# Two gated scan-and-experts layers: residual sums and normalisation statistics of the first five stages, VectorE's part given to TensorE and ScalarE

## What is computed

```python
x = x + tanh(g_xattn[0]) * scan0(ctx, layernorm(x))       # z gate = silu(layernorm(x))
x = x + tanh(g_ffn[0])   * experts(layernorm(x))          # 16 experts, 4 per row, and a shared one
x = x + tanh(g_xattn[1]) * scan1(ctx, layernorm(x))
x = x + tanh(g_ffn[1])   * lora(layernorm(x))

def layernorm(x, eps=1e-5):
    m, v = mean(x, -1), var(x, -1)
    return (x - m) / sqrt(v + eps)

# scan, for each of 512 channels and 16 states, along the 512 rows:
state = state * exp(d_t * A) + (d_t * u_t) * B_t;  y_t = sum_n state * C_t
y = (y + D * u) * silu(z)
# shared expert: silu(x @ gate.T) * (x @ up.T) @ down.T
```

## Time and profile before

| | |
|---|---|
| median of three runs | 1532.84 us |
| the profiled execution | 1534.31 us, its span 1532.5 us |
| VectorE busy | 1408.3 us, 92% |
| TensorE busy | 1270.7 us, 83% |
| ScalarE busy | 837.6 us, 55% |
| GpSimd busy | 786.1 us, 51% |
| TensorE's mean granted clock | 0.949 of full speed |

### The profile page before, as it was taken

How to read it: one execution, slowest core, us unless ns; L and a number is a source line. 1 busy time by engine, 2 the same in 40 slices (tenths; PEclk the granted TensorE clock), 3 DMA queues, 4 the chain that set the end, 5 groups by cost and what they waited for, 6 DMA issues and landing times.

```text
span 1532.5 us, 14502 instructions
## 1 busy us (share of the span) xinstructions
PE 1270.7 (83%) x4518; PEld 723.1 (47%) x4518; DVE 1408.3 (92%) x1468; ACT 837.6 (55%) x1344; POOL 786.1 (51%) x411
## 2 busy tenths in 40 slices
PE   6786787799689867986889999889988888836998
PEld 3321232343244324442456666566665666625555
DVE  5899999999999999998899999999899999987894
ACT  5755657464766455634865655647556444424442
POOL 0465456545544553450464555654556656555642
PEclk9898899999989998998999999999999999967999
DMA  7354445445543543451256768676786768754531
GB/s 251 103 135 128 111 130 143 130 120 143 139 139 92 145 130 107 96 165 29 83 177 239 236 239 273 231 273 236 248 258 231 280 268 280 247 191 141 169 106 56
DMA packets 99836, 264.30 MB, mean 172 GB/s; under 512 B 10832, under 2 KB 11344, under 8 KB 93616
## 3 DMA queue, kind: packets, MB, share of 16 engines
q1 hardware_dynamic: 87936, 225.36, 47.9%
q0 software_dynamic: 11440, 37.50, 7.3%
q10 hardware_dynamic: 384, 0.52, 0.1%
HBM read 233.73 MB, written 29.62 MB: 172 GB/s over the span
## 4 chain that ended last, share of the span: by engine, by line
DVE 41%; PE 24%; issue 8%; DMA 7%; POOL 5%; ACT 2%; DVEq 0%; SPq 0%; another core or an unknown queue 0%; ACTq 0%; POOLq 0%
DVE state L1663 18%; DVE banks L1655 11%; PE banks L1137 7%; DMA expert_w<-in_moe_w 3%; PE banks L1148 3%; PE banks L1047 3%; PE banks L1096 2%; DVE y_scan L1674 2%; DMA ys_d<-expert_out 2%; POOL state L451 2%; PE banks L1301 2%; PE banks L1104 1%; DVE hidden L1681 1%; DVE du L1375 1%; DVE small L1429 1%
## 5 line engine op out<-in xcount | busy, mean ns | idle before, releaser
L451 POOL TENSOR_TENSOR state<-state,bc_rows 128x1024 f32<-128x1024 f32 x254 | 599.0, 2359 | 641.9 <-DVE banks L1655 641.7
L1047 PE MATMUL banks<-state,ident 128*128 128x512 f32 x640 | 329.4, 645 | 115.5 <-POOL state L451 115.3
L1663 DVE TENSOR_TENSOR_SCAN state<-decay,banks 128x1024 f32<-128x1024 f32 x176 | 402.1, 2285 | 6.3 <-ACT decay L681 1.7
L1655 DVE TENSOR_TENSOR banks<-du,bc_rows 128x1024 f32<-128x1024 f32 x256 | 314.7, 1229 | 12.8 <-issue 0.5
L1137 PE MATMUL banks<-z_gate,expert_w 128*128 128x256 f32 (+1 forms) x1504 | 285.3, 348 | 7.6 <-DMA expert_w<-in_moe_w 7.3
L1137 PEld LDWEIGHTS banks<-z_gate,expert_w 128*128 128x128 f32 x1504 | 250.0, 191 | 60.8 <-issue 20.8
L681 ACT ACTIVATE decay<-delta,neg_a 128x511 f32<-128x511 f32 x352 | 230.8, 713 | 53.1 <-DVE state L1663 47.9
L1047 PEld LDWEIGHTS banks<-state,ident 128*128 128x128 f32 x640 | 118.3, 198 | 295.1 <-POOL state L451 184.3
L1663 DVE TENSOR_TENSOR_SCAN state<-expert_w,banks 128x1024 f32<-128x1024 f32 x80 | 182.9, 2286 | 8.5 <-ACT expert_w L681 5.9
L1148 PE MATMUL banks<-expert_w,hidden 128*128 128x512 f32 x316 | 155.2, 606 | 2.9 <-DVE hidden L1684 2.9
L1674 DVE TENSOR_TENSOR y_scan<-y_scan,state 128x1024 f32<-128x1024 f32 x94 | 113.9, 1212 | 3.1 <-POOL state L451 3.1
(11 more groups left out here) (313 smaller groups left out, 1622.8 us busy)
## 6 DMA issues: line engine op xcount, KB each, us to landing
bc_rows<-bc_d SPq DMA_DIRECT2D x208, 512.0 KB
expert_w<-in_moe_w SPq DMA_DIRECT2D x48, 1536.0 KB, 9.2
ys_d<-expert_out SPq DMA_DIRECT2D x32, 512.0 KB, 10.5
ctx_t<-in_ctxT SPq DMA_DIRECT2D x8, 512.0 KB, 6.8
x_res<-in_x SPq DMA_DIRECT2D x4, 1024.0 KB, 10.8
xn_d<-y_scan SPq DMA_DIRECT2D x4, 1024.0 KB, 7.5
ys_d<-expert_out SPq DMA_DIRECT2D x15, 256.0 KB, 9.3
out_x<-x_res SPq DMA_DIRECT2D x3, 1024.0 KB, 6.0
```

The source lines that it names most:

```text
L451: nc.gpsimd.tensor_tensor(W[:, c % 4], W[:, c % 4], bcast2(BC[:, u, 1, :]), ALU.mult).then_inc(mulc_done, 1)
L1047: mm = nc.tensor.matmul(PS[:, m], ID[:, :], W[:, c % 4, m, :], start=False, stop=True, skip_group_check=True)
L1655: nc.vector.tensor_tensor(drive(s), DU[:, s % 2, 2 * h:2 * h + 2, :], bcast2(BC[:, u, 0, :]), ALU.mult).then_inc(mulb_done, 1)
L1663: nc.vector.tensor_tensor_scan(flat(W[:, c % 4]), flat(DAS[c % da_slots(s, i)]), flat(drive(s)), 0.0, ALU.mult, ALU.add).then_inc(scan_don ...
```

## The change

- **TensorE adds the residual.** `y_transposes` becomes `scan_transposes` in stages 1 to 4: for each row tile an identity matmul puts the row tile of `x` into the bank, and four matmuls with the scan output as weights and `GID` (the identity times tanh of the gate) add the gated, transposed scan on top. `shared_out` likewise begins with an identity matmul of `x`; the shared expert's last weights are scaled by half the gate once, in place (`shw_ready`).
- **ScalarE copies out.** `scan_rows` copies each bank to `x` with a row sum as second output, scales the sums to negative means, and squares `x - mean` with a row sum of squares: the variance. It stands after c=5 and c=7 of the first quarter, ahead of `conv_tap(p, 1)` at c=5. `shared_rows` copies the shared banks to `x`, after c=0 and c=3 of the second quarter (stages 2, 3); in stage 4 after c=0 and c=2 of the second, and c=0 and c=2 of the third.
- **Input statistics.** `input_sums` (third quarter, c=0 and c=2), `mean` and `squares` (c=5, c=6) make those of the new batch.
- **VectorE** loses `scan_add`, `stats` and `shared_add` in these stages. `norm_bias` becomes a product for them, and EPS and 1/D go into `rstd_log` as bias and scale.

```diff
             def rstd_log(v):
                 act.wait_ge(var_ready, v + 1)
-                nc.scalar.activation(RS[:, :], RS[:, :], ACT.Ln).then_inc(std_step, 1)
+                nc.scalar.activation(RS[:, :], SQ[:, v % 2, :], ACT.Ln, scale=1.0 / D, bias=EPSC[:, :]).then_inc(std_step, 1)
+            def mean(v, lo, hi):
+                means[0] += 1
+                act.wait_ge(summed, means[0])
+                m = NMEAN[:, v % 2, lo:hi]
+                nc.scalar.activation(m, m, ACT.Copy, scale=-1.0 / D).then_inc(mean_ready, 1)
+            def squares(v, b, qs):
+                act.wait_ge(mean_ready, means[0])
+                for q in qs:
+                    ins = nc.scalar.activation(ZS[:, q, :], X[:, b * QT + q, :], ACT.Square, bias=NMEAN[:, v % 2, q:q + 1],
+                                               accum_out=SQ[:, v % 2, q:q + 1])
+                if q == QT - 1:
+                    ins.then_inc(var_ready, 1)
+            def input_sums(s, qs):
...
+                for q in qs:
+                    ins = nc.scalar.activation(ZS[:, q, :], X[:, s * QT + q, :], ACT.Copy, accum_out=NMEAN[:, 0, q:q + 1])
...
+            def scan_rows(f, lts):
+                for lt in lts:
+                    act.wait_ge(yt_done, QT * f + lt + 1)
+                    nc.scalar.activation(X[:, f * QT + lt, :], AUX[lt % 2], ACT.Copy,
+                                         accum_out=NMEAN[:, 1, lt:lt + 1]).then_inc(xacc, 1)
+                act.wait_ge(xacc, QT * f + lt + 1)
+                m = NMEAN[:, 1, lts[0]:lts[-1] + 1]
+                nc.scalar.activation(m, m, ACT.Copy, scale=-1.0 / D).then_inc(rows_mean, 1)
+                act.wait_ge(rows_mean, 2 * f + lts[-1] // 2 + 1)
+                for lt in lts:
+                    ins = nc.scalar.activation(ZS[:, lt, :], X[:, f * QT + lt, :], ACT.Square, bias=NMEAN[:, 1, lt:lt + 1],
+                                               accum_out=SQ[:, 1, lt:lt + 1])
...
+            def shared_rows(b, qs):
+                for q in qs:
+                    act.wait_ge(shdown_done, QT * b + q + 1)
+                    nc.scalar.activation(X[:, b * QT + q, :], AUX[q % 2], ACT.Copy).then_inc(shacc, 1)
...
+                    if c == 5 and f >= 0:
+                        scan_rows(f, (0, 1))
                     if c == (5 if f >= 0 else 6):
                         conv_tap(p, 1)
+                    if c == 7 and f >= 0:
+                        scan_rows(f, (2, 3))
...
                         decay(s, i, c)
+                        if i == 1 and c == 0 and g >= 0:
+                            shared_rows(g, (0, 1))
                         if i == 1 and c == 1:
                             silu_pair(p, 1)
+                        if i == 1 and c == 3 and g >= 0:
+                            shared_rows(g, (2, 3))
...
+                        if i == 2 and c in (0, 2):
+                            input_sums(s, (c, c + 1))
+                        if i == 2 and c == 5:
+                            mean(2 * s, 0, QT)
+                            squares(2 * s, s, (0, 1))
+                        if i == 2 and c == 6:
+                            squares(2 * s, s, (2, 3))
...
                 decay(s, 1, c)
+                if c == 0:
+                    shared_rows(f - 1, (0, 1))
                 if c == 1:
                     norm(f, XN)
+                if c == 2:
+                    shared_rows(f - 1, (2, 3))
...
+            def scan_transposes(f, y, lts):
+                pe.wait_ge(yg_done, f + 1)
+                pe.wait_ge(gid_ready, 1)
+                pe.wait_ge(ld_x[f], 16)
+                for lt in lts:
+                    if lt >= 2:
+                        pe.wait_ge(xacc, QT * f + lt - 1)
+                    nc.tensor.matmul(AUX[lt % 2], ID[:, :], X[:, f * QT + lt, :], start=True, stop=True)
+                    for et in range(ET):
+                        mm = nc.tensor.matmul(AUX[lt % 2][:, et * P:(et + 1) * P], y[:, et, lt * P:(lt + 1) * P], GID[:, :],
+                                              start=False, stop=True, skip_group_check=True)
+                    mm.then_inc(yt_done, 1)
...
                 for q in qs:
+                    nc.tensor.matmul(AUX[q % 2], ID[:, :], X[:, b * QT + q, :], start=True, stop=False)
                     for it in range(IT):
...
-                    if c == 4 and f >= 0:
-                        scan_add(f, (0, 1), 0)
-                    if c == 5 and f >= 0:
-                        scan_add(f, (2, 3), 0)
-                        dve.wait_ge(xacc, QT * (f + 1))
-                        stats(f)
-                    if c == 7 and g >= 0:
-                        shared_add(g, (0, 1))
...
-                        if i == 1 and c == 2 and g >= 0:
-                            shared_add(g, (2, 3))
```

63 lines of the change are left out of this document (34 added, 29 removed).

## The result

The changed kernel takes 1545.99 us, the median of six runs (1541.79 to 1548.43), against 1532.77 us for the kernel before in the same rounds (1530.36 to 1533.95): 1.0085 times as long, 95% interval 1.0072 to 1.0097. It is slower by about 13 us. Its profiled execution took 1548.34 us, span 1546.6, against 1534.31 and 1532.5 before: +14.1 us of span.

What follows compares the result with a forecast made beforehand. VectorE, 92% busy, was named the bound, but TensorE was as full where its new work lands. Stages 0 to 4 summed -3.0 + 0.6 + 2.9 + 1.0 + 7.6 = +9.1 us: 1542 us median, range 1522 to 1557.

Steps and rivals of the forecast that it cites:

- stage 4, second quarter: Scan c=3 starts at 678.9 instead of 671.35, its decay queued behind ScalarE's copy of shared rows: +7.6 us, nothing winning it back.
- TensorE's prices: A scan row tile costs 0.86 + 0.9 us against 0.43, a shared one 0.86 more; 35 us for TensorE in all.
- The lag and its way: TensorE's sums run 5.3 us late at scan c=6, 7.0 by the second quarter; VectorE's scans wait some 12 us a stage.
- The ends of stages 1 and 2: Last quarter into the next stage: TensorE is full, so VectorE's 3.0 us of freed statistics bring nothing; 0 each.
- Stage 2's middle: First quarter into the second: lag of +4.0 us, less the 1.07 us gap closed by VectorE arriving earlier, so +2.9.
- Stage 1's middle: VectorE's 5.8 us are eaten by the wait at c=6; the late convolution may cost up to 1.7 more: +0.6 us.
- Stage 4 behind the second quarter: Third quarter loses four shared adds on VectorE, TensorE gets 3.4 us before the index rounds: between -3 and +3, taken as 0.
- about 54 us: ScalarE's added work from copies, sums, squares and scalings, some 13 us a stage; accumulator outputs came on top.
- The cover of the third quarter: ScalarE's 6 to 8 us a stage hide in its waits there; without that cover, up to 3 us a stage.
- VectorE stays the bound: Rival: the ring of four states covers TensorE's lag, so VectorE's savings count; 1486 us in full, 1509 at half; 10%.
- It cancels: Rival: GID products as cheap as transposes, 3.5 us a stage instead of 5.3, and stage 4's block shorter; 1534 us; 20%.
- Square needs its own tables: Rival: each of four groups of squares a stage brings two 1.28 us table loads on ScalarE; 1560 us; 10%.

Runs made afterwards that it cites:

- e1: The changed kernel without the identity matmuls that add the residual, for scan and shared rows alike: 1520.97 us against 1534.34 for the kernel before, ratio 0.9914.
- e12: The changed kernel without the four identity matmuls per stage of the scan rows, the shared rows' kept: 1529.67 us against 1531.04 for the kernel before, ratio 0.9994.
- e2: The kernel before plus useless TensorE matmuls where the change adds work, VectorE and ScalarE keeping all theirs: 1562.61 us against 1534.34, ratio 1.0187.
- e7_warm: The changed kernel plus useless 128-column matmuls where TensorE waits before sums, in stages 1 to 3: 1539.64 us against 1532.0 for the kernel before, ratio 1.0053.
- e4_input_stats: The kernel before with only the input rows' statistics moved from VectorE to ScalarE: 1527.58 us against 1534.34, ratio 0.9959.
- e3: The changed kernel with stage 4's copy of shared row tiles 2 and 3 one decay later on ScalarE: 1541.57 us against 1534.34 for the kernel before, ratio 1.0046.
- e10: The changed kernel with useless matmuls in TensorE's waits in stages 1 to 3 and eight more in stage 4: 1540.92 us against 1534.15 for the kernel before.

## Why the prediction was right, and where its steps were off

The forecast was 1542 us in a range of 1522 to 1557, slower with a chance of 0.63; 1546.0 us came out. Between the two profiled executions, up to the first scan of stage 5:

| step | forecast | measured |
|---|---|---|
| stage 0 | -3.0 | -3.55 |
| stage 1, middle | +0.6 | +1.71 |
| stage 1, end | 0 | +2.35 |
| stage 2, middle | +2.9 | +3.98 |
| stage 2, end | 0 | +1.00 |
| stage 3, middle | +4.0 | +3.99 |
| stage 3, end | -3.0 | -2.76 |
| stage 4, second quarter | +7.6 | +7.61 |
| stage 4, from there on | 0 | +0.43 |
| sum | +9.1 | +14.8 |

(An end here runs from the end of the middle to the next stage, so that its measured value includes the 2.8 us of statistics that are gone; the ends of the table above begin behind them.)

- **TensorE's prices were right.** 1.75 us for a scan row tile against 0.43, 0.86 for a shared one. The whole came to 41.0 us busy instead of 35. The excess fits the new stretches at half clock, which count as busy (3.4 us at the end of stage 1, 3.2 in stage 4's router); it was not added up in full.
- **The lag and its way were right**, to 0.1 us in the two places where nothing else came in: stage 3's middle and stage 4's second quarter. The waits came at the scans named, 13.1 us where the text said some 12. That TensorE's load is the cause, and nearly in full on the path, is shown by e1, e12 and e2.
- **The ends of stages 1 and 2 failed.** I took them as fixed by TensorE, so that VectorE's 3 us there bring nothing. From scan c=4 of the last quarter on they became 5.1 and 3.8 us longer, 2.3 and 1.0 more than the 2.8 us of statistics account for. The step that failed is "TensorE is full there, 45.3 of 46 us": I priced its chain as if its clock could not change, though the same row has a clock of 0.93. Part of what looked full was slow. In the kernel before, at the end of stage 2:

```profile
435.14 4.53 PE L1083 MATMUL banks<-router_w,y_scan 128*128 128x16 f32 x32
439.51 3.76 PE L1047 MATMUL banks<-state,ident 128*128 128x512 f32 x4
```

  From the router's start to the end of the shared expert's first matmuls this is 15.7 us in both kernels. At the end of stage 1 it was 12.3, at full clock, and is 15.7 now. There the clock is 0.50 in a sum ahead of the transposes, 1.00 again from 287 to 293 us, and falls a second time inside the router, with no gap of TensorE since 289.2. The gaps ahead of that first sum (2.7, 2.8 and 1.7 us) are hardly other than before (2.7, 2.2 and 1.1), where one sum was at half clock too, at 280.82 us, and the router was not. Why the clock falls where it does was not settled. At the end of stage 2 the 1.0 us lies ahead of the router:

```profile
433.11 3.51 PE L1131 MATMUL banks<-state,ident 128*128 128x512 f32 x4 [3.02 <-POOL state L459]
```

  The same sum was 1.98 us before (at 428.60). The fillers of e7_warm give back 4.1 us in end 1 and 1.0 in end 2. With them the end of stage 1 would even have brought 1.7 us of the statistics' 2.8, and that of stage 2 none, as I wrote. The 1.0 us of stage 2 is not the price of TensorE's new work, since e4_input_stats has it without any. In e2_tensor_only, where TensorE kept its clock, both ends are 19.5.
- **Stage 2's middle** lacked the 1.07 us that I had credited to it. The gap did close (TensorE is busy 40.00 of 40 us), but not since VectorE came earlier: the end of stage 1 had eaten that lead. TensorE's first sums now start 4.0 us behind the stage's first scan, 2.3 before, and its first row tile starts 17.8 us behind it in both kernels. So the middle grows by 3.98 as in stage 3.
- **Stage 1's middle** was sized at +0.6 and is +1.71 here, +0.7 in two kernels with the same instructions up to there (e3, e7) and +1.9 in a third (e10). Here the first sum of the stage took 3.78 us and the convolutions behind it were at half clock in part (granted clock 0.58 from 180 to 185 us); in e3_stage4_later the sum took 3.37 and the convolutions were at full clock.
- **Stage 4 behind the second quarter** came to nearly 0 by two errors that cancel: routing +3.80, by the half clock behind the gap of 2.96 us, and -3.37 in the third and fourth quarter, where VectorE has no shared adds. I had given between -3 and +3 for the second and nothing for the first.
- **ScalarE**: "about 54 us", and the busy time grew by 54.9, but by luck. The list came to 54 without the accumulator outputs and to about 60 with the middle that I took for them; the new groups add up to 67. The growth of the busy time is smaller because instructions overlap and some records of the old work are missing from the later trace (184 decays for 188 in one group). Accumulator outputs are instructions of their own; I had taken the middle between 0 and 0.21, and they are 0.19 to 0.20:

```profile
L717 ACT ACTIVATE z_gate<-x_res,neg_mean 128x512 f32<-128x512 f32 x16 | 11.4, 714 | 0.3
...
L725 ACT ACTIVATE x_res<-banks 128x512 f32<-128x512 f32 x16 | 9.4, 593 | 35.4 <-PE banks L1205 35.4
...
L710 ACT ACTIVATION_READ_ACCUMULATOR x_res<-banks 128x1 f32 x16 | 3.2, 198 | 0.0
```

  The 35.4 us of idle of L725 are the time that ScalarE, in order, stands and waits for the shared expert's matmuls. The cover of the third quarter held, as e4_input_stats shows. On the rule that I weighed (the Trainium skill, ScalarE: Activation LUTs, Rules for kernel authors: adds on VectorE, said of bf16): here, in fp32, a plain bank copy at 593 ns is under VectorE's add at 733, one with its row sum at 593 + 198 is over it.
- **The rivals.** "VectorE stays the bound" is out: e1_no_identity, with TensorE almost at its old load, still waits 6.4 us in middle 3. "It cancels" needed cheap GID products; they cost full price. "Square needs its own tables" is out: no table load stands beside L717 or L692, and the loads of the other lines are as many as before within one. The Trainium skill (ScalarE: Activation LUTs, Table sets: the hidden batching unit) leaves square out of what it says is in every set; in this trace it ran beside exponentials with no load. The 0.09 us by which the Ln with a bias tile (297 ns) exceeds the one without (206) agree with the Trainium skill (ScalarE: Activation LUTs, What ACT_TABLE_LOAD costs), which gives about 93 ns for each such operand.

Of the 5.7 us between +9.1 and +14.8, 3.4 are the two ends and 2.2 the middles of stages 1 and 2. It didn't turn the sign.

## What to carry to other kernels

Read busy shares by stretch, not over the span: an engine with 17% of idle time overall had none in the stretch where the work was to go, and there what was given to it came out in the stage's length nearly in full (3.4 us for 3.4). Read the granted clock beside the busy share too: a stretch can be full because it is slow. Split a bundle by the engine that pays: the statistics, which only ScalarE paid for, were worth -14 us here, and the residual sums on TensorE turned that into +13. Where in-order queues hand work to each other, ask of each step what is behind it in the queue of the reader too; and where the trace shows TensorE at its lower clock anywhere near, give the sum a bound with the neighbouring work priced at that clock.
